# A pause on GpSimd behind every fourth gather of a four-layer graph-attention kernel

## The reference, cut to what matters

```python
wh = x @ W                                            # (4096, 64)
e = (wh @ a_src)[:, None] + (wh @ a_dst)[None, :]
e = leaky_relu(e, slope)                              # 0.2, 0.01, 0.2, 0.01
scores = jnp.where(adj > 0, e, NEG)
out = jax.nn.softmax(scores, axis=1) @ wh             # (+ bias), then elu
x = layernorm(x + out)
```

## Time and profile before

| | |
|---|---|
| time of the kernel, median of 3 runs | 600.63 us (600.36 to 600.85) |
| span of the profiled execution | 859.9 us |
| busy in it: PE, PEld, DVE, ACT, POOL | 419.1, 334.5, 349.6, 400.8, 278.0 us |
| mean granted TensorE clock in it | 0.815 |
| gathers | 292, 277.8 us of POOL |
| DMA | 84.86 MB, mean 99 GB/s |

### The profile page before, as it was taken

How to read it: one execution, slowest core, us unless ns; L and a number is a source line. 1 busy time by engine, 2 the same in 40 slices (tenths; PEclk the granted TensorE clock), 3 DMA queues, 4 the chain that set the end, 5 groups by cost and what they waited for, 6 DMA issues and landing times.

```text
span 859.9 us, 10681 instructions
## 1 busy us (share of the span) xinstructions
PE 419.1 (49%) x3453; PEld 334.5 (39%) x3453; DVE 349.6 (41%) x1601; ACT 400.8 (47%) x876; POOL 278.0 (32%) x296
## 2 busy tenths in 40 slices
PE   2354512246655786411129983310499633104985
PEld 1243301245543675300119862210397522004964
DVE  3035813744379598200003872300048622000587
ACT  2677612555476476200325971231269612313684
POOL 0000173140320410777710034777100437771000
PEclk9999999999999998555559995755599857555997
DMA  8999962482673100222200012222000112220000
GB/s 312 428 330 428 422 198 58 173 290 100 212 282 124 17 26 27 32 27 27 27 8 2 20 30 29 28 27 27 9 1 20 34 26 27 28 28 6 8 19 28
DMA packets 20546, 84.86 MB, mean 99 GB/s; under 512 B 6083, under 2 KB 11462, under 8 KB 16262
## 3 DMA queue, kind: packets, MB, share of 16 engines
q1 hardware_dynamic: 10102, 73.15, 21.8%
q0 software_dynamic: 9344, 9.89, 9.4%
q10 hardware_dynamic: 1040, 1.08, 0.4%
HBM read 78.72 MB, written 5.37 MB: 98 GB/s over the span
## 4 chain that ended last, share of the span: by engine, by line
another core or an unknown queue 23%; PE 17%; DVE 12%; ACT 11%; issue 9%; DVEq 0%; ACTq 0%
PE bank L709 7%; ACT arena L865 4%; PE bank L689 3%; PE bank L672 3%; ACT arena L851 2%; DVE x L1313 2%; PE bank L670 1%; DVE stats L1295 1%; PE bank L705 1%; ACT arena L875 1%; DVE arena L1232 1%; ACT arena L839 1%; PE bank L574 1%; DVE res L1292 1%
## 5 line engine op out<-in xcount | busy, mean ns | idle before, releaser
L528 POOL DMA_INDIRECT xg<-table,index x292 | 277.8, 951 | 499.4 <-DMA table<-wh 299.8
L1232 DVE CUSTOM_DVE_ANT_0 arena<-bank,arena 128x256 f32<-128x256 f32 (+3 forms) x123 | 63.4, 523 | 284.7 <-ACT arena L851 224.5
L851 ACT ACTIVATE arena<-bank,sloped_own 128x256 f32<-128x256 f32 (+3 forms) x123 | 68.5, 557 | 176.3 <-remote 109.7
L689 PE MATMUL bank<-packed,arena 128*128 128x128 f32 x339 | 68.3, 323 | 120.0 <-issue 74.0
L839 ACT ACTIVATE arena<-arena,half 128x4096 bf16<-128x4096 int32 x31 | 114.7, 3703 | 19.1 <-DMA arena<-in_adj_t 18.5
L689 PEld LDWEIGHTS bank<-packed,arena 128*128 128x128 f32 x339 | 46.0, 165 | 132.7 <-issue 118.5
L875 ACT COPY arena<-bank 128x256 f32<-128x256 f32 (+3 forms) x123 | 54.1, 446 | 75.4 <-remote 55.4
L670 PE MATMUL bank<-off_row,wall 128*128 128x256 bf16 (+3 forms) x132 | 43.9, 332 | 81.2 <-issue 58.4
L709 PE MATMUL bank<-xg,arena 128*128 128x64 f32 x486 | 73.0, 284 | 10.6 <-ACT arena L875 8.6
L709 PEld LDWEIGHTS bank<-xg,arena 128*128 128x128 f32 x486 | 63.7, 197 | 24.0 <-ACT arena L875 13.5
L1029 DVE MAX8 top<-bank 128x8 f32<-128x256 f32 x31 | 13.4, 431 | 131.5 <-remote 69.5
(11 more groups left out here) (148 smaller groups left out, 780.1 us busy)
## 6 DMA issues: line engine op xcount, KB each, us to landing
arena<-in_adj_t SPq DMA_DIRECT2D x31, 2048.0 KB
xg<-table,index POOLq DMA_INDIRECT x292
table<-wh SPq DMA_DIRECT2D x24, 132.0 KB, 1.7
arena<-in_adj SPq DMA_DIRECT2D x1, 2048.0 KB, 12.9
table<-wh ACTq DMA_DIRECT2D x1, 1056.0 KB
x<-in_x SPq DMA_DIRECT2D x1, 1024.0 KB, 15.0
out_x<-x SPq DMA_DIRECT2D x8, 128.0 KB, 1.9
packed<-in_c_packed SPq DMA_DIRECT2D x1, 312.0 KB
```

Source lines behind the costliest of these rows:

```text
L528: pool.indirect_dma_start(out=xg[:, c, :], out_offset=None, in_=table[l][0:rows, :], in_offset=bass.IndirectOffsetOnAxis(ap=index[:, c:c + ...
L689: t = nc.tensor.transpose(turned_ps[turned_bank(n)][:, c * P:(c + 1) * P], scores(l, n)[:, c * P:(c + 1) * P], ident[:, :])
L851: nc.scalar.activation(scores(l, n)[:, 0:m * P], score_ps[n % len(score_ps)][:, 0:m * P], ACT.Relu, bias=sloped_own[:, k:k + 1], scale=ALP ...
L1232: nc.vector.tensor_tensor_reduce(out=y, in0=score_ps[n % len(score_ps)][:, 0:m * P], in1=y, scale=-1.0, scalar=-FLOOR, op0=ALU.add, op1=AL ...
```

## The change

Behind every fourth gather, counted over all layers, POOL waits until the tile semaphore of that fourth gather has reached the full count of all gathers sent on it so far, that is, until that gather's rows (and earlier ones of the same tile) have landed. Nothing else is changed: the same 292 gathers in the same order, with 73 waits among them.

```diff
+BURST = 4
...
         def _(pool):
+            sent = [0] * TILES
+            burst = [0]
+
             def gather(l, k, c, rows=N):
                 pool.indirect_dma_start(
                     out=xg[:, c, :], out_offset=None, in_=table[l][0:rows, :],
                     in_offset=bass.IndirectOffsetOnAxis(ap=index[:, c:c + 1], axis=0),
                 ).then_inc(gathered[k], 16)
+                sent[k] += 1
+                burst[0] += 1
+                if burst[0] % BURST == 0:
+                    pool.wait_ge(gathered[k], 16 * sent[k])
```

## The result

The kernel with the waits takes 680.3 us (678.1 to 682.0, four runs) against 600.7 us before (600.4 to 601.7, four runs). The ratio is 1.1315, 95% interval 1.1283 to 1.1348: 79.6 us slower. The prediction said 653 us, between 610 and 690.

The account below looks back on a forecast made before the run. It took gathers and compute as close to balanced, with almost no slack on POOL. Waits added 21.6 us in layer 1 and 15.2 in each of layers 2 and 3, 52.0 on 600.6: 653 us, range 610 to 690.

Parts of the forecast that it names:

- The holds: Between PE and ACT while gathers are issued, a slope 11 us behind its matmuls; taken to belong to the profiled execution.
- the sum: Rebuilt time of the kernel before, 645.3 us; the median was 44.7 us lower, which layer 0 could give back.
- the price of a wait: On POOL behind every fourth gather: landing 2.37 us after its start plus restart, less a 1.25 us step; 1.2 us taken.
- the 0.30 us bound: POOL's semaphore and restart after a landing, put between nothing and the 0.30 us it idles between two gathers.
- where gathers bind: At a layer's end, through the last tile's rows: layer 1 bound by 4.6 us, layers 2 and 3 with 6.4 slack.
- T: End of the layer before, when ACT has copied the last `wh`; 347.8 us for layer 1 in the first profile.
- A: Gathers have slack and waits hide: POOL needs only 0.95 us per gather, only layer 1 grows, 611 us; chance 0.12.
- B: Holds between PE and ACT in layers 1 to 3 are partly real and pauses dissolve them: faster, 590 us; chance 0.04.
- C: Dearer: landings late by the 3.18 us row, 707 us, or PE's clock falling to half, 692 us; chance 0.10.

Follow-up runs that it names:

- Run 7: Kernel before, no waits, with 24 extra gathers of 128 rows into a spare tile ahead of layer 1's own: 630.3 us, ratio 1.0472.
- run 4: Kernel with the waits, each now on the latest tile whose gathers ended at least two gathers back, so rows have landed: 601.1 us, ratio 1.0023.
- run 3: Kernel with the waits, kept in layer 0 alone (18 of the 73): 601.1 us, ratio 1.0019.
- run 9: Kernel before, profiled again without any edit: 601.5 us for its one timed run, profiled execution of 599.6 us.
- run 10: Kernel with the waits, kept only among the first 20 gathers of layers 1 to 3 (5 in a layer): 628.3 us, ratio 1.0476.
- run 11: Kernel with the waits, kept only behind the later 53 gathers of layers 1 to 3: 652.2 us, ratio 1.0892.
- run 5: Kernel with the waits, kept in layer 1 alone (18): 626.9 us, ratio 1.0420.
- run 6: Kernel with the waits, kept in layer 2 alone (18): 624.7 us, ratio 1.0377.

## Why the prediction was right, and where it was off

**The direction and the range.** Gathers pace POOL at 1.25 us, POOL paces the layers but for some slack, and a pause on POOL beyond that slack is a pause of the kernel. Run 7 shows the pace in the timed run, run 4 that the landing is the price, run 3 that layer 0 hides its share. A loss of 52 us was forecast and 79.6 measured.

**The holds.** They were rightly read as no part of the timed run (run 9). Layer 0 gave back 51 us (347.8 to 296.8), where the sum wanted 44.7. One hold was read too short. The matmuls that end at 376.4 are tile 0's eighth segment, and the slope that starts at 387.4 is the seventh. The eighth starts here, 25 us after its matmuls:

```profile
401.40 0.69 ACT L851 ACTIVATE arena<-bank,sloped_own 128x512 f32<-128x512 f32 x1 [13.31 <-remote]
```

No term of the sum hangs on it.

**The term that was mis-sized: the price of a wait.** The prediction put 1.2 us, from rows 2.37 us after the start and almost nothing for the restart. It measured 1.77. The data is there sooner than I took it, 2.16 us in the wait shown, but 0.64 us then pass until POOL starts, more than twice the 0.30 us bound. Other waits take longer: layers 1, 2 and 3 average 1.74, 1.56 and 2.00 us. In most of the long ones the data comes later and the restart is about the same. Behind the gather that starts at 564.28 in layer 3 data moves for 3.20 us, and then nothing until POOL starts again:

```profile
567.48:568.05 0.57, 0.00 (x0) 0.00 (x0) 0.00 (x0) 0.00 (x0) 0.00 (x1) 1.00 0.00 0
```

With 1.77 in place of 1.2 the prediction's own sum is 31.9 + 2 x (31.9 - 6.4) = 82.9, against 79.6.

**The step that was wrong without showing in the sum: where gathers bind.** I had the last tile want its rows at T + 83.2 in every layer, so that they bind layer 1 from T + 87.8, and slack of 6.4 us at the ends of layers 2 and 3. In run 9 the last tile's matmuls start at T + 95.0, 84.4 and 82.1 in layers 1, 2 and 3: right for two layers, 12 us off in layer 1. In run 9's trace the last rows of layer 1 do come at about T + 87.9 (382.28 + 2.4 - 296.8), but they are not awaited. The layer is late from its head, where tile 1's rows came 10.3 us after PE wanted them. I had seen that place ("tile 1's third chunk lands near T + 17 instead of T + 12") and costed it inside the end's delay. In layer 1 the prediction's own terms have it before the change: the 20th gather starts at T - 4.6 + 19 x 1.25 = T + 19.2 with rows at T + 21.5, while the head has tile 1's slopes begin at T + 13.5. A delay there counts in full: run 10 lost 28.2 us with 15 waits there. In return, layer 1 has slack at its end, and the waits there hide 5 us in each layer (run 11). The two mistakes nearly cancel: 12.8 us of slack were forecast, and of the waits' 95.4 us all but 78.2 (79.6 less the 1.4 of layer 0) were hidden, so 17. The total is near by luck, since its split was wrong: none was forecast for layer 1, where run 5 paid 25.2 of 31.4 us.

**The rivals.** A is refuted by run 7. B, that pauses free something, found no support: run 9 has no holds to free. C is partly there. The tail of a layer, from the last tile's matmuls to the last copy of `wh`, with TensorE's granted clock behind POOL's busy time. Layer 1 of after, of run 9 and of run 5:

```profile
419.48:435.39 15.91, 11.38 (x43) 8.69 (x42) 8.54 (x44) 5.63 (x21) 8.56 (x9) 0.50 0.20 36
...
391.82:405.41 13.59, 7.78 (x44) 5.38 (x42) 8.89 (x48) 5.99 (x24) 10.41 (x11) 0.83 0.27 47
...
417.14:430.71 13.57, 7.67 (x44) 5.39 (x42) 9.00 (x48) 5.89 (x24) 10.22 (x12) 0.78 0.27 47
```

Layer 2 of after, of run 9 and of run 6:

```profile
538.85:554.78 15.93, 11.38 (x43) 8.68 (x42) 8.88 (x44) 6.31 (x23) 9.03 (x10) 0.50 0.22 36
...
489.85:504.15 14.30, 8.31 (x44) 5.81 (x42) 9.08 (x48) 6.67 (x26) 10.95 (x12) 0.73 0.25 46
...
512.12:528.06 15.94, 11.39 (x43) 8.69 (x42) 8.81 (x45) 6.32 (x23) 12.17 (x13) 0.50 0.27 45
```

At 0.50 (1.2 GHz) throughout, the tail takes 15.9 us, against 13.6 in layer 1 and 14.3 in layer 2 at a higher clock: 2.3 and 1.6 us that no term of mine had. Run 5 has the same 18 waits in layer 1 as after, and its tail is as short as before at 0.78. In run 6 no wait on POOL falls into the tail of layer 2, and at 0.50 it is as long as in after. So the tail goes with the clock and not with the waits of its own layer. Why the clock stayed at half in one and not in the other is open.

**The forecasts for the trace.** An idle time of 1.5 us behind every fourth gather was forecast, and 1.7 us or more are there. The 90 us of layer 1 became 121, not 112. POOL was to start layer 2 about 1 us before the last tile's matmuls, and starts 2.8 us before (416.69 against 419.48). The profiled span was to be no verdict, and it was none against the first profile.

## What to carry to other kernels

A wait for the last DMA on the engine that issues it costs the landing and the restart, less one issue step, each time; if that engine paces the kernel, look which of its items is awaited first, because a delay at the head of a layer counts in full while one at the end may find slack. Before reading waits out of a profile, compare its span with the timed median; when they are far apart, profile again. And an order that fills idle time with early work can put the urgent item behind it: 12 early gathers moved back in layer 1 (and 3 in the others) brought 6 us.

## What the runs showed that was not expected

The same kernel had profiled spans of 859.9 and 599.6 us, with a handover from PE to ACT that took 25 us in the first and no such hold in the second. The cause was not found; no run brought the long one back.

A gather whose data has moved 2.16 us after its start let POOL start the next one 0.64 us later. And the landing varies from gather to gather: a wait cost 1.56 us on average in layer 2 and 2.00 us in layer 3. It is no noise of one run. The 18 steps with a wait in layer 1 of run 5 are within 0.2 us of those in after, and the step behind the 17th gather of layer 3 is 3.77 us both in after and in run 10:

```profile
568.05 0.95 POOL L532 DMA_INDIRECT xg<-table,index  x1 [2.82 <-DMA xg<-table,index]
...
535.57 0.94 POOL L532 DMA_INDIRECT xg<-table,index  x1 [2.83 <-DMA xg<-table,index]
```

The waits stand behind other chunks in each layer, because 73 is no multiple of four. Whether a long landing comes from the chunk or from what else happens at that place is not shown.
